# Twelve sublayers on one core: keys and values of the long attention made inside the mixture, one output bank per batch, and delta-rule masks per half batch

## The reference

```
# mixture (L2 ffn): top-1 of 8 experts, at most CAPACITY tokens each
top1 = argmax(logits);  rank = position of the token among those of its expert
dispatch[top1, slot] += tokens;  h = gelu(dispatch @ wi);  out = weight * (h @ wo)[top1, slot]
# delta rule (L3 attn), per batch, W0 = 0, over the 100 tokens
y_t = W q_t;  err = W k_t - v_t;  W = W - 0.01 * err k_t^T
# long attention (L3 xattn): 16 query heads, 4 key heads, width 8
k = ctx @ Wk;  v = ctx @ Wv;  attn = softmax(q k^T / sqrt(8)) over 1444 keys;  out = (attn v) @ Wo
```

## Time and profile before

| | |
|---|---|
| device time, median of 3 runs | 1231.24 us (1228.54 to 1233.5) |
| device time of the profiled execution | 1233.62 us |
| its span | 1232.1 us |
| busy in the span | PE 939.7, DVE 757.7, ACT 561.1, POOL 262.8 us |
| mixture | about 762 to 839 us of the span |
| delta rule | about 839 to 913 us |
| long attention | about 913 to 1206 us |

### The profile page before, as it was taken

The page is one execution under the profiler, slowest core; times in us unless marked ns, Lnnn a source line. Parts: engine busy times, 40 slices in busy tenths (PEclk is TensorE's granted clock), DMA queues, the critical chain, the costliest instruction groups (busy, mean ns, idle before and its releaser), DMA issues. The chain is left out here.

```text
span 1232.1 us, 18660 instructions
## 1 busy us (share of the span) xinstructions
PE 939.7 (76%) x6239; PEld 580.7 (47%) x6239; DVE 757.7 (61%) x2185; ACT 561.1 (46%) x1643; POOL 262.8 (21%) x356
## 2 busy tenths in 40 slices
PE   5975799999697262689758797376766999999985
PEld 2344688889555130435533466263751233333333
DVE  6548677777556595545677355104556888888833
ACT  3236477777442100313435223231133777777773
POOL 4006255554300112213020000250013111111100
PEclk8697799999898685659768699595775899999998
DMA  9500000000001601000001002400005222111000
GB/s 230 130 2 1 1 2 2 2 2 2 1 0 26 82 0 18 9 1 1 1 12 36 1 1 63 118 25 1 1 21 107 42 43 42 43 39 40 3 1 14
DMA packets 76129, 35.85 MB, mean 29 GB/s; under 512 B 35274, under 2 KB 74513, under 8 KB 76034
## 3 DMA queue, kind: packets, MB, share of 16 engines
q1 hardware_dynamic: 73666, 33.61, 12.4%
q0 software_dynamic: 896, 0.63, 0.2%
q10 hardware_dynamic: 1472, 0.41, 0.2%
HBM read 24.42 MB, written 11.05 MB: 29 GB/s over the span
## 5 line engine op out<-in xcount | busy, mean ns | idle before, releaser
L453 DVE TENSOR_REDUCE L3x_NMP<-L3x_pM 128x1 f32<-128x361 f32 x384 | 179.6, 525 | 33.6 <-PE L3x_pM L681 33.3
L564 ACT ACTIVATE L3x_E<-L3x_pS 128x400 f32<-128x400 f32 (+1 forms) x384 | 170.2, 506 | 53.9 <-PE L3x_pS L703 53.3
L681 PE MATMUL L3x_pM<-ctx_tm 64*128 64x361 bf16 x384 | 101.3, 340 | 19.1 <-DMA ctx_tm<-query_terms 9.6
L1559 ACT ACTIVATE L0x_E<-L0x_E,ctx_r 128x100 f32<-128x100 f32 x288 | 105.0, 369 | 9.1 <-DVE L0x_E L1466 9.1
L703 PE MATMUL L3x_pS<-ctx_tm 64*128 64x400 bf16 (+1 forms) x384 | 103.2, 349 | 2.8 <-ACT L3x_E L564 2.7
L720 PE MATMUL L3x_pO<-L3x_E,ctx_tm 128*32 128x400 f32 (+1 forms) x768 | 85.3, 516 | 0.0
L681 PEld LDWEIGHTS L3x_pM<-ctx_tm 64*128 64x128 bf16 x384 | 28.8, 97 | 114.2 <-DVE L3x_NMP L453 80.5
L1648 PE MATMUL L0x_pU<-ctx_tm,L0x_E 128*100 128x129 f32 (+1 forms) x576 | 74.5, 282 | 3.0 <-POOL L0x_E L1379 3.0
L1648 PEld LDWEIGHTS L0x_pU<-ctx_tm,L0x_E 128*100 128x100 f32 (+1 forms) x576 | 67.7, 170 | 8.0 <-POOL L0x_E L1379 3.8
L1638 PE MATMUL L0x_pS<-L0x_QS,CT 128*128 128x100 f32 x576 | 70.1, 280 | 0.0
L1379 POOL TENSOR_TENSOR L0x_E<-L0x_E,L0x_RZ 128x1200 f32<-128x1200 f32 x24 | 52.6, 2192 | 76.2 <-DVE L0x_RZ L1486 76.2
(11 more groups left out here) (626 smaller groups left out, 2161.3 us busy)
## 6 DMA issues: line engine op xcount, KB each, us to landing
ctx_tm<-in_ctx SPq DMA_DIRECT2D x8, 704.0 KB
key_terms<-L3x_KT SPq DMA_DIRECT2D x48, 90.2 KB
ctx_tm<-key_terms SPq DMA_DIRECT2D x16, 270.8 KB, 4.5
ctx_tm<-in_L_ffn_wi SPq DMA_DIRECT2D x4, 512.0 KB, 7.5
ctx_tm<-in_L_ffn_wo SPq DMA_DIRECT2D x4, 512.0 KB, 7.7
query_terms<-ctx_tm SPq DMA_DIRECT2D x12, 100.0 KB, 2.1
ctx_tm<-query_terms SPq DMA_DIRECT2D x16, 75.0 KB, 4.7
slots_in<-L2a_zeros SPq DMA_DIRECT2D x8, 129.0 KB
```

What stands on the lines that cost most here:

```text
L453: nc.vector.tensor_reduce(NMP[:, p, i // NC4, a, i % NC4:i % NC4 + 1], v, AX.X, ALU.max, negate=True).then_inc(s_mr, 1)
L564: nc.scalar.activation(E[0:r, n % EB, :], pS[0:r, n % 3, 0:NG * T], ACT.Exp, scale=SCALE8).then_inc(s_e, 1)
L681: nc.tensor.matmul(pM[:, n % 3, 0:CW], key_rows(QS, a)[:, b, p, 128 * x:128 * x + 128], key_rows(KS, a)[:, b % KB, c, p, :], start=True, s ...
L1559: last = nc.scalar.activation(E[:, n % 3, k, :], E[:, n % 3, k, :], ACT.Exp, scale=m.ctx_r[:, n % B, k:k + 1], accum_out=Z[:, n % 2, k:k + 1])
```

## The change

1. Keys and values of the long attention, for all 8 batches, are made in the mixture, in its own PSUM banks (two for keys, two for values), on PE, ACT and DVE; the terms are written to DRAM there (48 DMAs on SP between the loads of `L2f_XS` and the gather). KP, VP and VT are gone from the timetable. The rows of batches 0 to 2 are read back during the delta rule.
2. In the long attention one output bank takes both pairs of heads of a batch, with one ACT copy in place of two. `token_major` goes in halves of 2 products at steps 48 and 50 in place of 4 products at 47 and 48 each; NT0 moves from 15 to 16, TURN to 56, PROJ to 60.
3. Queries are made in three parts (100, 300 and 400 tokens), each term by one DMA (9 in place of 12); the rows of batch 0 are read as soon as part 0 is written. Fills of ones and zeros and the reordering of query weights move from the head of the long attention into the delta rule, on ACT.
4. In the delta rule K·K and K·Q of four batches share a bank and come before the values; ACT copies K·K to SBUF; DVE masks 4 batches per operation, POOL makes levels 1 to 6 of the masks; the values follow the first level's T products, with the bias added by DVE.

```diff
--- before.py
+++ after.py
...
+def long_buffers(nc, m):
...
+    v.KT = part((B - 1) * 3 * (CW + 1), BF16).rearrange("p (b n x) -> p b n x", b=B - 1, n=3)
...
+    v.V = m.CT[:, :, :].rearrange("p b (k a x) -> p b k a x", k=NKT, a=2)
...
-    KP_AT, VP_AT, VT_AT, NT0_AT, NT1_AT, TM_AT, TURN_AT, PROJ_AT = 6, 8, 11, 15, 28, 48, 50, 52
+    NT0_AT, NT1_AT, TM_AT, TURN_AT, PROJ_AT = 16, 28, (48, 50), 56, 60
...
+        PARTS = [(0, T), (T, HALF), (HALF, TOK)]
...
-                key_writes(0)
-                query_writes(0)
-                key_rows_back(0)
-                query_rows(0)
-                query_writes(1)
+                for i in range(len(PARTS)):
+                    if i >= 1:
+                        sp.wait_ge(s_qd, 48 * i)
+                    for term in (1, 2, 3):
+                        query_write(i, term)
+                    if i == 0:
+                        query_rows(0)
                 for b in range(1, B):
                     query_rows(b)
-                    key_writes(b)
-                    key_rows_back(b)
+                    if b >= KB:
+                        key_rows_back(b)
...
-                            nc.tensor.matmul(pO[r:r + 32, 0:NG * T], V[0:NW[k], b % 2, k, 2 * p + a, :],
-                                             E[0:NW[k], n % EB, :], start=(g == 0), stop=(g == 5),
-                                             skip_group_check=True).then_inc(s_pv, 1)
...
+                            nc.tensor.matmul(pO[r:r + 32, 0:NG * T], V[0:NW[k], b, k, a, 16 * p:16 * p + 32],
+                                             E[0:NW[k], n % EB, :], start=(p == 0 and g == 0),
+                                             stop=(p == 1 and g == 5), skip_group_check=True).then_inc(s_pv, 1)
+
+                def token_major(b, part):
...
+                    for g in range(2 * part, 2 * part + 2):
+                        last = nc.tensor.matmul(pP[0:T, 0:D + NH], OC[:, g * T:(g + 1) * T],
...
+                for b in range(B):
+                    sp.wait_ge(s_k3, b + 1)
+                    for term in (1, 2, 3):
+                        key_write(sp, m.long.kd, KT(b, term), b, term, s_kd)
...
+                for b in range(B):
+                    dve.wait_ge(s_k1, b + 1)
+                    nc.vector.tensor_tensor(XK[:, b % 2, :], pY[:, b % 2, 0:CW], KT(b, 1), ALU.subtract)\
+                      .then_inc(s_xk, 1)
+                    dve.wait_ge(s_vp, b + 1)
+                    nc.vector.memset(V[:, b, :, :, 16:16 + HD + 1], 0.0)
+                    nc.vector.memset(V[:, b].rearrange("r k a (p x) -> r (k a p) x", x=32)[:, :, HD], 1.0)\
+                      .then_inc(s_vz, 1)
+                    dve.wait_ge(s_k2, b + 1)
+                    nc.vector.tensor_tensor(KT(b, 3), XK[:, b % 2, :], KT(b, 2), ALU.subtract).then_inc(s_k3, 1)
...
+                def value_columns(b):
+                    act.wait_ge(s_vt, b + 1)
+                    act.wait_ge(s_vz, b + 1)
+                    src = turned_values(b).rearrange("r (k u d) -> r k u d", k=NKT, d=HD)
+                    dst = V[:, b].rearrange("r k a (p x) -> r k (a p) x", x=32)[:, :, :, 0:HD]
+                    nc.scalar.copy(dst[:, 0:8], src[:, 0:8])
+                    nc.scalar.copy(dst[0:NW[8], 8:NKT], src[0:NW[8], 8:NKT]).then_inc(s_vc, 1)
...
+                for b in range(B):
+                    act.wait_ge(s_kp, b + 1)
+                    nc.scalar.copy(KT(b, 1), pY[:, b % 2, 0:CW]).then_inc(s_k1, 1)
+                    act.wait_ge(s_vp, b + 1)
+                    if b >= 2:
+                        act.wait_ge(s_vt, b - 1)
+                    nc.scalar.copy(VX[:, b % 2, :], pC[:, b % 2, 0:CW]).then_inc(s_vx, 1)
+                    if b >= 1:
+                        value_columns(b - 1)
+                    act.wait_ge(s_xk, b + 1)
+                    nc.scalar.copy(KT(b, 2), XK[:, b % 2, :]).then_inc(s_k2, 1)
+                value_columns(B - 1)
...
+                def projected(b):
+                    if b >= 2:
+                        pe.wait_ge(s_xk, b - 1)
+                    for c in range(NC4):
+                        last = nc.tensor.matmul(pY[32 * c:32 * c + 32, b % 2, 0:CW],
+                                                wkp[:, :, :, :].rearrange("r a d i -> r (a d i)"),
+                                                m.CT[:, b, c * CW:(c + 1) * CW], start=True, stop=True,
+                                                skip_group_check=True)
+                    last.then_inc(s_kp, 1)
+                    if b >= 2:
+                        pe.wait_ge(s_vx, b - 1)
+                    for c in range(NC4):
+                        last = nc.tensor.matmul(pC[32 * c:32 * c + 32, b % 2, 0:CW],
+                                                wvp[:, :, :, :].rearrange("r a i d -> r (a i d)"),
+                                                m.CT[:, b, c * CW:(c + 1) * CW], start=True, stop=True,
+                                                skip_group_check=True)
+                    last.then_inc(s_vp, 1)
+
+                def values_turn(b):
+                    pe.wait_ge(s_vx, b + 1)
+                    if b >= 2:
+                        pe.wait_ge(s_vc, b - 1)
+                    for x in range(3):
+                        n = NW[4 * x]
+                        last = nc.tensor.transpose(turned_values(b)[0:n, 128 * x:128 * x + 128],
+                                                   VX[:, b % 2, 128 * x:128 * x + n], m.ident[:, :])
+                    last.then_inc(s_vt, 1)
...
+                pe.wait_ge(s_kw, 1)
+                projected(0)
                 pe.wait_ge(s_oh, 1)
...
+                for b in range(1, B):
+                    projected(b)
+                    values_turn(b - 1)
+                values_turn(B - 1)
+                pe.wait_ge(s_vc, B)
+                pe.wait_ge(s_xk, B)
...
+                for l in range(1, NL):
+                    for h in range(2):
+                        pool.wait_ge(s_kc, h + 1)
+                        nc.gpsimd.tensor_tensor(LT[:, l, h * HB:(h + 1) * HB, :], KK[:, h],
+                                                each_batch(m.below[0:T, l + 1, 0:T]), ALU.mult).then_inc(s_lt, 1)
...
+                    dve.wait_ge(s_kc, h + 1)
+                    nc.vector.tensor_tensor(X[:, h], KK[:, h], each_batch(m.below[0:T, 0, 0:T]), ALU.mult)
+                    chain.then(nc.vector.tensor_tensor(LT[:, 0, h * HB:(h + 1) * HB, :], KK[:, h],
+                                                       each_batch(m.below[0:T, 1, 0:T]), ALU.mult))
...
+                for h in range(2):
+                    act.wait_ge(s_kk, 2 * h + 1)
+                    nc.scalar.copy(KK[:, h], batches(pC, h)).then_inc(s_kc, 1)
                 for n in range(2 * (NL - 1)):
+                    if n == 2:
+                        key_ones(0)
+                    if n == 4:
+                        key_ones(1)
+                    if n == 6:
+                        key_ones(2)
+                    if n == 8:
+                        query_zeros(0, 3)
+                    if n == 10:
+                        query_zeros(3, 6)
...
+                query_zeros(6, B)
+                query_weights()
...
+                def values():
...
+                        pe.wait_ge(s_lt, n + 1)
+                        if n < 2:
+                            pe.wait_ge(s_x0, 2 * h + 1)
...
+                    if l == 1:
+                        values()
+                        pe.wait_ge(s_x0, 4)
```

447 lines of the change are left out of this document (193 added, 254 removed).

## The result

The changed kernel took 1191.39 us (median of 4 runs, 1189.43 to 1193.37), the one before 1231.06 us (4 runs, 1228.54 to 1233.5): a ratio of 0.9677, 95% interval 0.9649 to 0.9704, or 39.7 us less. 1190 was predicted, with 1180 to 1204 around it. The profiled execution of the changed kernel is the fastest of its four (span 1187.7 us).

What follows compares the result with a forecast made beforehand. PE was taken to set the loop's pace (28.19 of 31 us), with the mixture a chain of transfers. Mixture +1, delta rule −11.3, head −8.5, loop −3.0 −17.4 −1.5 −1.1 sum to −41.8: 1190 us, range 1180 to 1204.

Steps and rivals of the forecast that it cites:

- Loop: Long attention's loop and its tail: less PE work saves 2.9 us a batch, −23.0 us in the sum, bounds −16 to −27.
- token-major part: Loop's two token-major steps a batch: half of the products in each saves 1.2 us, taken as 1.1 a batch.
- key projection's 1.4 us: Loop: removing the next batch's key projection saves 1.4 us a batch, read from batch 7, which has none.
- Head: Long attention, norm to first loop product: query rows written and read earlier, 8.5 us saved, between 7 and 10.
- Delta rule: Delta rule's head: XX starts 12.3 us earlier, less 1 for DVE beside POOL; net −11.3, between −9 and −14.5.
- if DVE's masks take over 1 us: Delta rule: a sign that the prediction is wrong; DVE's masks of 100x400 were forecast at 0.56 us each.
- Mixture: Key and value work under PE's wait for scattered tokens: ACT's chain ends last, cost +1 us, bounds −1.5 and +8.
- The clock's rise: Mixture: PE's clock rises early in the added work; with experts starting at full clock the bound is −1.5 us.
- rival 1: Mixture's wait isn't free: longer scatters or PE at half clock make +6 to +8 instead of +1, 1196; chance 0.16.
- rival 2: Delta rule's head: DVE's and POOL's masks block each other, +6 us, giving 1196; chance 0.12.
- Rival 3: Loop held by something else (DVE, late maxima's terms, bank queue): only 1.6 to 1.8 a batch, 1198; chance 0.12.
- the slower case: Loop: with less PE work the clock might fall to half, making the kernel over 100 us slower; chance 0.03.

Runs made afterwards that it cites:

- both dummies: Changed kernel with two dummy projections a batch put back into the long attention at steps 6 and 11, without DVE's read between: 1198.36 us (0.9723).
- queries in halves: Changed kernel with queries in two parts of 400 tokens in place of three of 100, 300 and 400: 1195.73 us, one execution.
- NT0: Changed kernel with the first turn of the maxima at step 15 of a batch in place of 16: 1190.57 us, one execution.
- shifted: Changed kernel with 24 more transposes of the router weights ahead of the first one of the mixture: 1191.64 us, one execution.
- closer dummies: Changed kernel with dummy projections at steps 6 and 8, DVE's read of the bank between, PROJ at 62 in place of 60: 1204.06 us (0.9732).
- the last version: Changed kernel with POOL's later masks held until DVE has made its own, and the three table reductions ahead of the queries: 1186.72 us (0.9629).

## Why the prediction was right, point by point

*Loop, −23.0 predicted, −21.6 measured.* From the first reduction of batch 1 to that of batch 7 it is 188.8 us before and 171.4 after, −17.4 as forecast. Batch 0 gave 4.1 us by DVE's reductions (933.5 to 963.0, now 911.1 to 936.4), more than the 3.0, but 1.7 of that was lost ahead of its first reduction, which the sum had missed. The end, from batch 7 on, gave 1.8 where 2.6 were forecast. The split was right for the token-major part (1.1; shown: 1.0). The key projection's 1.4 us was read from the kernel before, whose batch 7 lacks that job; of it 1.2 us is the one step in which PE waits 1.20 us for the bank. So the reason is mostly that wait: both dummies without it were worth 0.45 us a batch. Put back by the dummies was 0.7 for the key projection and 0.3 for the value one. Of the 2.8 us a batch, then, 2.0 is shown by putting work back (2.6 with the job that had to move). The rest, which holds the turning of the values, the single output bank and the moved steps, was not taken apart; the prediction had priced the turning at 0.1 and the single bank at nothing.

*Head, −8.5 predicted, −9.9.* The read landed in 2.5 us (906.47 to 908.95), not in the 4.7 taken from a read that had stood behind others; the write before it was slower than its 1.8 (the term was written at +4.7, the read went out at +7.1). By DVE's first reduction the head is worth 8.3, of which queries in halves took back 0.5; that the rest comes from the key work and the fills that no longer stand in front is read from the rows, and no run took it apart.

*Delta rule, −11.3 predicted, −13.1.* No run undid the earlier K·K products; the 11.5 us by which XX comes earlier are read from the rows. XX came when forecast, by luck: two errors cancelled. The clock was at 2.4 GHz through the K·K and K·Q products (16 in 3.1 us, forecast 5.4), so T started 1.2 us earlier in the stage than forecast (14.6, not 15.8), and DVE and POOL cost 2.7 us between the halves, where 1 stood in the sum. One of the prediction's own signs of being wrong came true here, "if DVE's masks take over 1 us" (1.28 to 1.40), and the sum held in spite of it. The rest of the stage gained 1.5 us more, which the sum did not have: the first level's XX products took 2.82 us at 2.4 GHz, and before 4.71:

```profile
876.18:880.89 4.71, 4.71 (x34) 4.71 (x33) 1.05 (x2) 0.49 (x1) 0.00 (x0) 0.58 0.02 3
```

*Mixture, +1 predicted, +2.2 in this profile.* The number is near and the mechanism wasn't the forecast one. The forecast had ACT's chain end last, 1 us behind the tokens, in every execution. In the four traces without gaps (NT0, shifted, closer dummies, and the last version) neither ACT nor PE ended last: their work hid under the wait, and the experts started on the tokens, at 28.0 to 28.7 us. The stage took 76.9 to 77.7 us, much as the 77.55 before. In the eight others with all the work ACT's chain or PE's did end last, but some 4 us later than the tokens had come in the four, since the fourth and fifth batch came late: the experts started at 31.9 to 33.3.

The clock's rise had been put into the forecast, and it comes only with the late start. Where the experts follow the key and value work within 0.9 us (the eight traces with gaps) they run at 1.00, and PE is busy 30.4 to 30.8 us with their 208 instructions in place of 31.9 before. In the four without gaps PE waits 1.1 to 2.0 us for the tokens, the clock falls to 0.50 soon after the start, PE is busy 31.8 to 32.1 us, and from the experts' start the stage takes 48.7 to 49.1 us, against 48.7 before: nothing is given back.

The 48 key writes ended at 818.1, 9 us ahead of the gather's read at 827.5. The end was forecast to the microsecond, but again by two errors: they began at 786.4 and not at 790, and took 0.66 us each and not 0.57.

So rival 1, the wait that isn't free, holds in eight traces of twelve, but not for its reasons. The scatters were not longer, and they start at the same times to 0.4 us in traces with gaps and without. Half clock isn't the main part: behind the gap one batch ran at it in the changed kernel (3.3 us in place of 1.8), but four traces without such a batch start their experts at most 0.3 us earlier (31.9 to 32.1). Where such batches came later, the start was 0.8 to 1.2 us later still (32.9 and 33.3).

*The other rivals.* DVE and POOL do slow each other: rival 2's mechanism was real, at 1.5 us of the stage (2.3 by the means of the traces) and not 6. Four masks took 4.1 us in the first half and 5.0 in the second, in place of 2.3 each, so DVE lost 1.8 and 2.7 us, where the rival had 3.6 in the first half alone. Rival 3 is refuted by the batch of 28.65 us, and NT0 at 15 gave nothing. The loop's clock stayed at 1.00 with PE busy 26.78 of 28.65 us: nothing of the slower case.

What stays open: the cause of the gaps, which the forecast had no term for and which make up all of the mixture's loss. In all eight traces PE's gap stands behind the fifth value projection, and ACT starts on the fifth batch's keys 5.0 to 5.8 us after their row's end, where in the four it is 0.1. But a kernel with the same instructions up to there had neither, and one packet of the instruction queue came in those microseconds in traces with gaps and without. PE's results are on time again from about 25.4 us into the stage, when SP's read of the scattered tokens goes out too; whether the two are linked isn't shown. And of the key projection's price before, 1.4 us, only a half was rebuilt.

## What to carry to other kernels

When one repetition of a loop lacks a job (here the last batch's key projection), its steps price that job with all its waits, better than the job's own busy time does: four products of 0.8 us in all cost 1.4 us here, most of it a wait for a bank that two engines read in turn. Work moved into a wait was free where it ended before the wait did (four traces), and paid back through PE's clock only where the next products followed it within 0.9 us. Products made 2.2 us earlier gained nothing here, since the clock was then down. And a sum that comes out right should be checked term by term: twice here two errors cancelled.

## What had not been expected of the hardware

- Masks of 100x400 with two operands in SBUF took 0.56 us on DVE alone, and 0.84 to 1.40 beside POOL's; POOL's went from 1.0 to 1.2 us. The mask with one operand in PSUM took 0.56 us beside POOL's too.
- The same 16 f32 products (32 instructions) took 2.8 us at 2.4 GHz and 5.2 at a mean of 0.53.
- In the four traces without gaps the clock was at 1.00 when PE began to wait for the tokens, and within 2 us of the experts' start it was at 0.50, though the wait was only 1.1 to 2.0 us. Behind waits of 0.7 to 0.9 us it stayed at 1.00.
- A read of query rows landed in 2.5 us with nothing ahead of it in the queue, 5.1 with others.
- PE stood 1.3 to 2.7 us with no semaphore named, at one place of the program, in eight of twelve traces with the full work, and ACT got its results up to 5.8 us after their rows' ends.
